# Attention scores accumulated by differences of key tiles, banks released one by one, an exponential placed behind the last Gelu

## The chip, the cores and the metric

The kernel runs on one core of a Trainium2 chip. The metric is the device time of one execution in microseconds, from launch to end; the profile's span is the time from the first to the last instruction and is a little shorter. The core has a matrix engine (TensorE, PE in the rows; PEld are its weight loads), a vector engine (VectorE, DVE), an activation engine (ScalarE, ACT), GpSimd (POOL) and SyncE (SP), which here issues all transfers. The engines run their own instruction lists and wait for each other through semaphores.

## What is computed

Two transformer layers on x of shape 4 x 1024 x 256, all in float32. The first layer is the one that most of the change touches:

```
x = x + attention_0(layernorm(x))     # 8 heads of 64, keys and values from a latent of 64
x = x + ffn_0(layernorm(x))           # silu gate, two hidden layers of 1024 with exact gelu
x = x + attention_1(layernorm(x))     # 16 heads of 16, rotary positions
x = x + ffn_1(layernorm(x))           # silu gate, 768 hidden
# attention_0:
scores = einsum('bqhd,bkhd->bhqk', q, k) * 64 ** -0.5
attn = softmax(scores, axis=-1)
out = einsum('bhqk,bkhd->bqhd', attn, v)
```

## The kernel before

There are two blocks of code. `attention_a` is the first attention, from 0 to about 787 us. `ffn_attention_ffn` holds the rest: it runs the first feed-forward layer block by block, the second attention, and the last feed-forward layer. The change touches `attention_a` in most places and the second block in one.

`attention_a` absorbs the key projection into the query, so all heads use the same latent of 64 numbers per token as keys. `Kh` and `Kl` hold it as a rounded high part and the rest (type fp32r, one pass on TensorE), for 1024 tokens of one of the 4 batches, in two copies, one for partitions 0 to 63 and one for 64 to 127, so that two heads run side by side. The same holds for the queries `Qh`, `Ql`.

The work is cut into units `u` (32 of them: 4 batches, 4 pairs of heads, 2 halves of 512 queries), each of 8 key tiles `t` of 128 keys, done in 4 pairs `j` (`t` = 2j and 2j+1). For each key tile:

- `scores(n)` (L969) makes keys x queries for both heads in the two banks of `psS[n % 2]`: four terms of two matmuls each, `Kh Qh`, `Kh Ql`, `Kl Qh`, and `spread` times `M`. The last subtracts the row's maximum: `M` has it in one row per head. Tile `t` uses the same two banks as tile `t-2`.
- `exponent(n)` on ScalarE (L589) makes `P` out of the banks; `weigh(n)` multiplies it with the values, in plain fp32; VectorE (`add`, L742, L746) and GpSimd (L885, L888, L892) add up `P` for the softmax's denominator.
- Six pairs ahead, `maxima(n)` (L945) makes queries x keys with the high parts alone in two banks of `psX`, and VectorE's `reduce(n)` (L709) takes the maximum over keys: with one instruction over two neighbouring banks (L720), or with two where the two banks are the last and the first (L722, L723).

`psX` has three banks that go round as a ring: `x_order` (L327) lists every user in the order of TensorE. A maximum takes two places (`double`), the others one: queries (in j=0), sums (end of j=1), rows and the output projection (j=2), and some more. A user waits until the one that had its bank before has released it. A double key had one release, when both heads had been reduced. The first 12 maxima partly use `psS`, which is still empty (`early_banks`).

In a pair TensorE's order is: a maximum, two key tiles of scores, the second maximum, the pending output projection (12 matmuls of 256 columns), the query (6 matmuls), latents and values of the next batch, `max_rows`, layer norm turns, then `weigh` for the two tiles of the pair before, and the sums. VectorE's order is: the first maximum, the additions of the pair before (L742 in j=3, L746 in j=0), one step on a weight tile (in turn, over four pairs: load, rounding on ScalarE, L771 which subtracts the rounded part, L774 which reduces it; from unit 22 on five steps with a cast L768), the second maximum, then what is left. The weight tile steps run on VectorE in j=1 and j=2 in the four-step form.

The denominator goes round through memory: sums on TensorE, a copy, a DMA, a reciprocal on VectorE in j=2, two DMAs, then GpSimd's `scale_out` (L876) on the output of that unit. The `wt` tiles in `shared` are weight buffers of the next block, filled by three loads at the end of SyncE's list in `attention_a` (L537).

In the second block ScalarE's list has, step by step `H`, the exponentials of the second attention (L1704), `leave(key)` for the feed-forward results (Silu at L1761, Gelu at L1765 and L1766, a scaled copy at L1770) and other copies. Where a function needs another table than the loaded one, an ACT_TABLE_LOAD stands in front of it.

## Time and profile before

| | us |
|---|---|
| median of the timed runs (three) | 2405.14 |
| lowest, highest | 2404.36, 2409.79 |
| the profiled execution | 2402.36 |
| its span | 2400.6 |
| TensorE busy | 2331.3 (97%) |
| VectorE busy | 1504.9 (63%) |
| ScalarE busy | 1342.5 (56%) |
| GpSimd busy | 1046.5 (44%) |

The shares are means over stages of different kinds; what a change in one stage is worth is read from that stage. The table of stretches gives for chosen stretches how long each engine was busy, with the number of instructions, then TensorE's granted clock as a part of full speed. The grouped instructions show, after the engine, operation, output and inputs, the count, the busy time, the mean of one in ns, and the idle time before them with the one that ended it. In a timeline a row begins with its start and its length; an idle time before it and its releaser stand in brackets. A row of matmuls marked x2 or x8 is several in one. TensorE's matmuls are pipelined and their ends are modelled, so the distance between starts tells what one costs, not its length.

### The profile page before, as it was taken

The page shows a single profiled execution, that of the slowest core. Times are in us where ns is not written, and L with a number is a line of the kernel's source. Part 1 is how long each engine was busy: PE and PEld are TensorE (multiplying, and loading weights), DVE is VectorE, ACT ScalarE, POOL GpSimd, SP SyncE. Part 2 cuts the span into 40 slices and gives each one's busy share as a digit, 9 for nine tenths or more (in the row PEclk, how much of TensorE's full clock was granted, in tenths as well). Part 3 has the DMA queues.
Part 4 walks back from the last instruction along what each step waited for, and adds up shares of the span by engine and source line. Part 5 has one row for each costly group of instructions (what it writes and reads, how often), then busy time and mean ns, then how long its engine had stood idle before and what let it go on. Part 6 is the DMA issues. An engine that isn't in the chain of part 4 may idle for free.

```text
span 2400.6 us, 39029 instructions
## 1 busy us (share of the span) xinstructions
PE 2331.3 (97%) x15265; PEld 1449.8 (60%) x15265; DVE 1504.9 (63%) x1938; ACT 1342.5 (56%) x1783; POOL 1046.5 (44%) x674
## 2 busy tenths in 40 slices
PE   6989999999999999999999999999999999999999
PEld 4545555555555788888888887444444444444588
DVE  6877777787784224322222223779989989989364
ACT  3555555554444444444444443478778778777743
POOL 1656776766677346556556556130000000000354
PEclk8999999999999999999999999999999999999999
DMA  2111321221212455565565556433333323322232
GB/s 61 63 69 54 98 79 56 98 65 61 73 44 69 149 167 181 176 196 184 172 197 185 173 188 201 128 90 80 88 79 72 86 77 75 90 79 55 61 121 80
DMA packets 156836, 259.04 MB, mean 108 GB/s; under 512 B 37004, under 2 KB 97292, under 8 KB 156300
## 3 DMA queue, kind: packets, MB, share of 16 engines
q1 hardware_dynamic: 156652, 256.53, 35.7%
q8 instruction: 123, 2.02, 0.3%
q14 instruction: 61, 0.50, 0.1%
HBM read 206.52 MB, written 60.68 MB: 111 GB/s over the span
## 4 chain that ended last, share of the span: by engine, by line
PE 62%; ACT 2%; DVE 1%; DMA 1%; issue 1%; SPq 1%; POOL 0%; POOLq 0%
PE m_R L129 46%; PE m_O L129 11%; PE m_X L129 4%; ACT m_P L1704 1%; DMA m_K<-bounce_k 1%; PE m_X L226 1%; ACT m_OS L1711 1%; DVE m_mraw L1853 0%; SPq L1562 0%; PE m_X L2067 0%; DVE m_ln_x L205 0%; PE m_R L226 0%; DMA inverses<-m_rinv 0%; DVE m_ln_stat L183 0%; SPq L1589 0%
## 5 line engine op out<-in xcount | busy, mean ns | idle before, releaser
L1853 DVE TENSOR_REDUCE m_mraw<-m_R 128x2 f32<-128x1024 f32 x512 | 622.6, 1221 | 71.1 <-PE m_R L129 57.6
L1704 ACT ACTIVATE m_P<-m_R 128x1024 f32<-128x1024 f32 x512 | 523.5, 1025 | 149.6 <-PE m_R L129 149.2
L589 ACT ACTIVATE a_P<-a_S 128x1024 f32<-128x1024 f32 x256 | 248.7, 1023 | 214.5 <-PE a_S L129 213.6
L129 PE MATMUL m_O<-m_P,m_V 128*17 128x256 f32 x4096 | 330.1, 394 | 4.5 <-ACT m_P L1704 2.6
L888 POOL TENSOR_TENSOR a_accp<-a_accp,a_P 128x1024 f32<-128x1024 f32 x96 | 251.9, 2624 | 15.3 <-ACT a_P L589 6.1
L1958 POOL TENSOR_TENSOR m_act0l<-m_xf,m_act0h 128x512 fp32r<-128x512 f32 x128 | 164.8, 1290 | 210.6 <-ACT m_xf L1766 111.2
L129 PE MATMUL a_O<-a_P,a_V 128*64 128x512 f32 x1024 | 247.7, 605 | 4.4 <-ACT a_ON L597 4.4
L129 PE MATMUL m_R<-m_act0h,wt 128*128 128x512 f32 x640 | 251.5, 393 | 0.0
L129 PE MATMUL m_R<-m_act0l,wt 128*128 128x512 f32 x640 | 250.4, 391 | 0.0
L720 DVE TENSOR_REDUCE a_mraw<-a_X 128x2 f32<-128x1024 f32 x164 | 199.7, 1218 | 79.6 <-PE a_X L129 79.5
L129 PE MATMUL m_R<-m_Q,m_K 64*128 64x512 f32 x800 | 200.6, 498 | 2.3 <-DVE m_mraw L1853 2.0
L129 PE MATMUL m_R<-m_act1l,wt 128*128 128x512 f32 x512 | 202.1, 395 | 0.0
L129 PE MATMUL m_R<-m_act1h,wt 128*128 128x512 f32 x512 | 200.8, 392 | 0.0
L129 PE MATMUL m_R<-m_K,m_Q 48*128 48x512 f32 x800 | 181.7, 450 | 4.8 <-ACT m_P L1704 3.7
L1982 POOL TENSOR_TENSOR m_ON<-m_ON,m_yt 128x512 f32<-128x512 f32 x16 | 20.5, 1283 | 377.0 <-DMA m_yt<-inverses 377.0
L129 PE MATMUL m_R<-next_hi,wt 128*128 128x512 f32 x424 | 168.9, 398 | 2.8 <-PEq L40 2.8
L129 PEld LDWEIGHTS m_O<-m_P,m_V 128*17 128x17 f32 x4096 | 85.3, 121 | 139.6 <-issue 130.0
L129 PE MATMUL m_R<-next_lo,wt 128*128 128x512 f32 x424 | 168.4, 397 | 0.0
L129 PEld LDWEIGHTS m_R<-m_Q,m_K 64*128 64x128 f32 x800 | 74.6, 183 | 151.2 <-issue 127.6
L129 PEld LDWEIGHTS m_R<-m_act0h,wt 128*128 128x128 f32 x640 | 120.2, 188 | 26.8 <-POOL m_act0l L1958 2.1
L129 PEld LDWEIGHTS m_R<-m_act0l,wt 128*128 128x128 f32 x640 | 120.3, 188 | 24.4 <-issue 0.5
L129 PE MATMUL a_X<-a_Kh,a_Qh 64*128 64x512 f32 x496 | 113.7, 450 | 19.2 <-DVE a_mraw L720 11.9
(251 smaller groups left out, 4235.0 us busy)
## 6 DMA issues: line engine op xcount, KB each, us to landing
wt<-wcopy SPq DMA_DIRECT2D x176, 512.0 KB, 3.4
m_K<-bounce_k SPq DMA_DIRECT2D x96, 128.0 KB, 5.4
m_ln_x<-x SPq DMA_DIRECT2D x23, 512.0 KB, 4.0
a_tile<-in_L_ffn_tiles SPq DMA_DIRECT2D x22, 512.0 KB, 4.5
wcopy<-in_L_ffn_tiles SPq DMA_DIRECT2D x22, 512.0 KB, 5.2
x<-xres SPq DMA_DIRECT2D x78, 128.0 KB, 3.2
m_Q<-bounce_q SPq DMA_DIRECT2D x150, 64.0 KB, 2.2
xres<-x SPq DMA_DIRECT2D x64, 128.0 KB, 2.6
```

The source lines that it names most:

```text
L129: return pe.eng.matmul(out, lhsT, rhs, start=start, stop=stop, skip_group_check=True)
L226: ins = pe.eng.transpose(bank[:, 128 * k:128 * k + 128], self.x[:, 4 * half + k, 128 * f:128 * f + 128], ident)
L589: act.eng.activation(P[n % NP][:, :, :], psS[n % 2][:, :, :], ACT.Exp, scale=SCALE).then_inc(s_exp)
L720: dve.eng.tensor_reduce(mraw[u % 2][:, t, :], psX[:, first:first + 2, :], AX.X, ALU.max).then_inc(X.free(key))
L888: pool.eng.tensor_tensor(accp[:, :, :], accp[:, :, :], P[n % NP][:, :, :], ALU.add).then_inc(s_addp)
L1704: act.eng.activation(P[h % 4][:, :, :], pair(key)[:, :, :], ACT.Exp, scale=SCALE).then_inc(R.free(key))
L1711: act.eng.activation(OS[:, :], psO[:, :], ACT.Copy).then_inc(s_os)
L1853: dve.eng.tensor_reduce(mraw[u % 2][:, at, :], pair(key)[:, :, :], AX.X, ALU.max).then_inc(R.free(key))
L1958: pool.eng.tensor_tensor(act_buf[dst][1][:, m, :], xf[fs(key) % 2][:, :], f32(act_buf[dst][0][:, m, :]), ALU.subtract).then_inc(s_lo)
L1982: pool.eng.tensor_tensor(ON[:, f, cols], ON[:, f, cols], yt[half][:, :], ALU.mult).then_inc(s_norm[half])
```

## The change

Three things. First, the scores of tiles t >= 2 are no longer made anew. `differ(b, half)` on TensorE makes K_t - K_{t-2} for tiles 2 to 7 of a batch, with the identity and its negative as weights: `half` 1 is 256 columns (tiles 6, 7), `half` 0 is 512 (tiles 2 to 5). ScalarE rounds it into `Dh`, which lies in the `wt` buffers, and VectorE writes the rest over `Kl`. `scores` then adds three terms to what stands in the banks since tile t-2, without the flag that starts a sum and without the `spread` term. For a later batch the two halves are made in j=3 of units 6 and 7 of the batch before; for the first, ahead of the loop. The loads into `wt` wait for the last scores that use the buffer. Second, a maximum has one ring key for each head, and VectorE reduces and releases each bank by itself. Third, a 4-column Exp is issued behind the last Gelu of the first feed-forward layer.

```diff
+    def differ_at(u, j):
+        b = u // UB + 1
+        return (b, {(6, 3): 1, (7, 3): 0}[u % UB, j]) if b < B and (u % UB, j) in ((6, 3), (7, 3)) else None
...
-            out += [("max", n), ("max", n + 1)] if n < STEPS else []
+            out += [("max", n + i, h) for i in range(2) for h in range(NH)] if n < STEPS else []
...
-        X = Ring(p, "x", 3, x_order(), double=("max",))
+        X = Ring(p, "x", 3, x_order())
...
+        Dh = [shared.wt[i][:, 0:T - 256] for i in (0, 1, 0, 2)]
...
+        def differ_cols(half):
+            return slice(768, T) if half else slice(256, 768)
+
+        def differ_back(half):
+            return slice(512, 768) if half else slice(0, 512)
...
             for i in range(3):
                 sp.wait_ge(s_copy, 16 * LOWS0)
+                sp.wait_ge(s_scores, (3 * UB * NT, 2 * UB * NT, STEPS)[i])
                 sp.eng.dma_start(f32(shared.wt[i][:, :]), wcopy[i]).then_inc(s_wt, 16)
...
+            def differ_high(b, half):
+                key, cols = ("differ", b, half), differ_back(half)
+                act.wait_ge(*X.filled(key))
+                if b >= 2:
+                    act.wait_ge(s_scores, NT * UB * (b - 1))
+                act.eng.activation(Dh[b][:, cols], differ_bank(key), ACT.Copy).then_inc(s_differ)
...
+            act.eng.activation(minus[:, :], ident[:, :], ACT.Copy, scale=-1.0).then_inc(s_identr)
...
+            def differ_low(b, half):
+                key, cols = ("differ", b, half), differ_cols(half)
+                dve.wait_ge(s_differ, 2 * b + 2 - half)
+                dve.eng.tensor_tensor(Kl[b % 2][:, cols], differ_bank(key), f32(Dh[b][:, differ_back(half)]), ALU.subtract).then_inc(X.free(key))
...
-                    dve.wait_ge(*X.filled(key))
-                    first = X.slot(key)
-                    if first < 2:
-                        dve.eng.tensor_reduce(mraw[u % 2][:, t, :], psX[:, first:first + 2, :], AX.X, ALU.max).then_inc(X.free(key))
-                    else:
-                        dve.eng.tensor_reduce(mraw[u % 2][:, t, 0:1], max_bank(n, 0), AX.X, ALU.max)
-                        dve.eng.tensor_reduce(mraw[u % 2][:, t, 1:2], max_bank(n, 1), AX.X, ALU.max).then_inc(X.free(key))
+                    for h in range(NH):
+                        key = ("max", n, h)
+                        dve.wait_ge(*X.filled(key))
+                        dve.eng.tensor_reduce(mraw[u % 2][:, t, h:h + 1], bank(key), AX.X, ALU.max).then_inc(X.free(key))
...
+            def differ(b, half):
+                key, here, back = ("differ", b, half), differ_cols(half), differ_back(half)
+                pe.wait_free(X, key)
+                pe.wait_ge(s_identr, 2)
+                for i in range(2):
+                    pe.wait_ge(*X.emptied(("latent", b, i)))
+                terms = [(identr[:, :], k[b % 2][:, here]) for k in (Kh, Kl)] + [(minus[:, :], k[b % 2][:, back]) for k in (Kh, Kl)]
+                products(pe, differ_bank(key), terms).then_inc(X.full(key))
...
                 if early_banks(n) is None:
-                    pe.wait_free(X, key)
+                    for h in range(NH):
+                        pe.wait_free(X, ("max", n, h))
...
-                terms = ((Kh[b % 2], cols, Qh[u % 3]), (Kh[b % 2], cols, Ql[u % 3]), (Kl[b % 2], cols, Qh[u % 3]), (spread, slice(0, 128), M[u % 3]))
+                if t < 2:
+                    terms = ((Kh[b % 2], cols, Qh[u % 3]), (Kh[b % 2], cols, Ql[u % 3]), (Kl[b % 2], cols, Qh[u % 3]), (spread, slice(0, 128), M[u % 3]))
+                else:
+                    for half in range(2):
+                        pe.wait_ge(*X.emptied(("differ", b, half)))
+                    since = slice(128 * t - 256, 128 * t - 128)
+                    terms = ((Dh[b], since, Qh[u % 3]), (Dh[b], since, Ql[u % 3]), (Kl[b % 2], cols, Qh[u % 3]))
                 for i, (w, c, x) in enumerate(terms):
                     for h in range(NH):
                         rows = slice(64 * h, 64 * h + 64)
-                        ins = mm(pe, psS[n % 2][:, h, :], w[rows, c], x[rows, :], i == 0, i == 3)
+                        ins = mm(pe, psS[n % 2][:, h, :], w[rows, c], x[rows, :], t < 2 and i == 0, i == len(terms) - 1)
...
+                    if key == ("hidden", NB - 1, 1, MT - 1):
+                        act.wait_ge(norm.s_half, 1)
+                        act.eng.activation(ready[:, :], norm.minus_half[:, :], ACT.Exp)
```

## Rows read from the trace of the kernel before

**Rows 1.** Table of stretches: length, then busy us of each engine, clock, DMA
```profile
200.00:560.00 360.00, 354.25 (x2286) 201.35 (x2282) 274.36 (x346) 191.67 (x252) 258.95 (x114) 1.00 0.24 77
560.00:700.00 140.00, 131.82 (x855) 73.91 (x857) 109.85 (x124) 66.27 (x85) 95.48 (x43) 1.00 0.21 65
```

**Rows 2.** Grouped instructions by shape, 25 to 755 us
```profile
L720 DVE TENSOR_REDUCE a_mraw<-a_X 128x2 f32<-128x1024 f32 x164 | 199.7, 1218 | 79.6 <-PE a_X L129 79.5
...
L129 PE MATMUL a_S<-a_M,a_spread 64*128 64x512 f32 x500 | 99.7, 391 | 0.0
...
L771 DVE TENSOR_TENSOR a_tile<-a_tile,a_tile_hi 128x1024 f32<-128x1024 f32 x22 | 38.8, 1762 | 4.8 <-ACT a_tile_hi L643 4.8
```

**Rows 3.** Timeline of TensorE over one unit: j=2, then j=3, 0, 1
```profile
300.96 0.50 PE L129 MATMUL a_X<-a_Kh,a_Qh 64*128 64x512 f32 x2
...
301.99 0.39 PE L129 MATMUL a_S<-a_M,a_spread 64*128 64x512 f32 x2
302.22 0.39 PE L129 MATMUL a_S<-a_Qh,a_Kh 64*128 64x512 f32 x2
...
303.68 0.28 PE L129 MATMUL a_X<-a_wo,a_osp1l 128*128 128x256 f32 x1
303.80 0.40 PE L129 MATMUL a_X<-a_wo,a_osp1h 128*128 128x256 f32 x2
...
307.19 0.50 PE L129 MATMUL a_X<-a_Kh,a_Qh 64*128 64x512 f32 x2
...
311.56 0.51 PE L129 MATMUL a_X<-a_Kh,a_Qh 64*128 64x512 f32 x2
...
314.66 0.63 PE L129 MATMUL a_X<-a_ln_hi,a_wq 128*128 128x512 f32 x2
...
317.55 0.50 PE L129 MATMUL a_X<-a_Kh,a_Qh 64*128 64x512 f32 x2
...
322.49 0.50 PE L129 MATMUL a_X<-a_Kh,a_Qh 64*128 64x512 f32 x2
```

**Rows 4.** Timeline of VectorE: one early place, then pair j=1 of that unit
```profile
89.33 3.04 DVE L771 TENSOR_TENSOR a_tile<-a_tile,a_tile_hi 128x1024 f32<-128x1024 f32 x1
...
318.09 1.23 DVE L720 TENSOR_REDUCE a_mraw<-a_X 128x2 f32<-128x1024 f32 x1 [0.98 <-PE a_X L129]
319.23 1.25 DVE L771 TENSOR_TENSOR a_tile<-a_tile,a_tile_hi 128x1024 f32<-128x1024 f32 x1
320.40 0.68 DVE L722 TENSOR_REDUCE a_mraw<-a_X 128x1 f32<-128x512 f32 x1
321.00 0.67 DVE L723 TENSOR_REDUCE a_mraw<-a_X 128x1 f32<-128x512 f32 x1
```

**Rows 5.** Waits of TensorE, 40 to 757 us: total, times, longest
```profile
PE a_X L129 <- DVE a_mraw L720: 12.3, 16, 1.8
```

**Rows 6.** Timelines ahead of the loop: VectorE, then TensorE
```profile
35.48 1.23 DVE L715 TENSOR_REDUCE a_mraw<-a_S 128x2 f32<-128x1024 f32 x1 [1.10 <-PE a_S L129]
...
40.20 0.80 PE L129 MATMUL a_X<-a_Kh,a_Qh 64*128 64x512 f32 x2 [2.64 <-DVE a_mraw L715]
```

**Rows 7.** Timelines: GpSimd's last addition of a unit, TensorE's sums of it
```profile
317.00 2.39 POOL L892 TENSOR_TENSOR a_accd<-a_accd,a_accp 128x1024 f32<-128x1024 f32 x1
...
321.93 0.64 PE L129 MATMUL a_X<-a_accd,a_ones 128*32 128x256 f32 x8
```

**Rows 8.** Timeline of TensorE: the closing sums of the first attention
```profile
772.67 1.08 PE L129 MATMUL a_X<-a_accd,a_ones 128*64 128x512 f32 x4 [0.70 <-issue]
```

**Rows 9.** Start of the second attention's exponentials: ScalarE, TensorE, the stretch
```profile
1528.93 1.28 ACT L1704 ACT_TABLE_LOAD   x1
1530.23 2.88 ACT L1704 ACTIVATE m_P<-m_R 128x1024 f32<-128x1024 f32 x3
...
1531.30 0.50 PE L129 MATMUL m_R<-m_K,m_Q 48*128 48x512 f32 x2 [1.75 <-ACT m_P L1704]
...
1530.00:1535.00 5.00, 3.51 (x20) 1.44 (x20) 2.90 (x4) 3.09 (x4) 0.00 (x0) 0.76 0.53 209
```

More of the change, by code:

```diff
@@ L331, in x_order @@
         for n in range(2 * AHEAD):
-            out += [("max", n)] if early_banks(n) is None else []
-            out += [("rows", 0)] if n == NT - 1 else []
+            out += [("max", n, h) for h in range(NH)] if early_banks(n) is None else []
+            out += [("differ", 0, 1), ("differ", 0, 0), ("rows", 0)] if n == NT - 1 else []
         pending = None
@@ L419, in bank, with differ_bank @@
             return psX[:, X.slot(key), :]
+        def differ_cols(half):
+            return slice(768, T) if half else slice(256, 768)
+        def differ_back(half):
+            return slice(512, 768) if half else slice(0, 512)
+        def differ_bank(key):
+            return bank(key)[:, 0:256] if key[2] else bank(key)
         def max_bank(n, h):
@@ L423, in max_bank @@
                 return psS[early_banks(n)][:, h, :]
-            return psX[:, (X.slot(("max", n)) + h) % 3, :]
+            return bank(("max", n, h))
         def p_freed_by_adds(n):
@@ L643, in tile_high @@
                 act.eng.activation(tile_hi[:, :], tile[:, :], ACT.Copy).then_inc(s_tile_hi)
+            for half in (1, 0):
+                differ_high(0, half)
             keep_rows(0)
@@ L817, in vector @@
                 reduce(n)
+                if n == NT - 1:
+                    for half in (1, 0):
+                        differ_low(0, half)
             pending = None
@@ L960, in maxima @@
                     ins = mm(pe, max_bank(n, h), Qh[u % 3][rows, 128 * q:128 * q + 128], kt[rows, 512 * kh:512 * kh + 512])
-                ins.then_inc(X.full(key) if early_banks(n) is None else s_early)
+                    if early_banks(n) is None:
+                        ins.then_inc(X.full(("max", n, h)))
+                if early_banks(n) is not None:
+                    ins.then_inc(s_early)
             def max_rows(u):
@@ L1048, in tensor @@
                 if n == NT - 1:
+                    for half in (1, 0):
+                        differ(0, half)
                     max_rows(0)
```

17 lines of the change are left out of this document (14 added, 3 removed).

## Prediction

> **What bounds the kernel now.** I read first the table of stretches. In the steady part of the first attention TensorE is busy 354.25 of 360 us at the full clock (1.00, the 2.4 GHz level), VectorE 274.36 (76%), ScalarE 53%, GpSimd 72%. In the stretch where weight tiles are cast (560 to 700 us) TensorE has fallen to 131.82 of 140 and VectorE is at 78% [rows 1]. So TensorE bounds this stage, with VectorE close behind. Next the grouped instructions: the term `spread`/`M` is 500 recorded matmuls, two per key tile (32 units of 8 tiles make 512) [rows 2]. Then the timeline. Two matmuls of the two heads run side by side: such a couple starts 0.23 us after the one before (301.99 to 302.22). From it come the lengths of the four pairs of a unit, by the first maximum of each: j=2 6.23 us (300.96 to 307.19), j=3 4.37, j=0 5.99, j=1 4.94, together 21.53 [rows 3]. Last, who waits for whom: between 40 and 757 us TensorE waited 12.3 us in 16 places for a whole maximum (L720) [rows 5]; these are the places where VectorE already rules.
>
> **The change part by part.**
>
> **Scores by differences.** From t=2 on a key tile adds (K_t - K_{t-2})Q to the bank that still holds the scores of t-2, whose subtracted maximum stays in it. Three couples are left of four. 6 of 8 tiles of 32 units are 192 tiles: 192 x 0.23 = **44.2 us** less TensorE work. Pairs j=1, 2, 3 lose 0.46 each, j=0 (t=0, 1) none. That this comes off the span holds only while TensorE is what ends last.
>
> **Making the differences.** Per batch `differ` adds four matmuls of 512 columns and four of 256, all with 128 rows. Two of the 512-column kind in a row take 0.63 us at 314.66, where one alone is 0.39 [rows 2, 3]: 0.23 to 0.24 for each more, as a couple. Two of 256 columns follow each other in 0.12 (303.68 to 303.80) [rows 3]. So 4 x 0.23 + 4 x 0.12 = 1.4 us, in three batches inside the loop 4.2 us. Ahead of it the engine changes from 64 to 128 rows, some 0.1, which the matmuls behind it paid before. ScalarE (two copies) is 53% busy and hides its part. VectorE gets two subtractions per batch, some 0.35 and 0.6 us, in j=3, where only the add L742 stands beside the maxima; the following maximum needs them at about 4.8 us of a pair that the same `differ` has lengthened, so nothing.
>
> **Before the loop** `differ(0)` falls between maximum 7 and `max_rows(0)`. VectorE is the bound there: TensorE waits 2.64 us for it at 40.20. But VectorE idles 1.10 us before 35.48 [rows 6]; the two subtractions (0.95) fit into most of that. Bounds -0.5 (a busier TensorE could leave the 1.2 GHz level earlier) to +1.5; I take +0.3.
>
> **Releasing banks singly.** 164 maxima that were one L720 of 1218 ns become two reductions [rows 2]; the other 84 after the early ones were already split. In the chain one L720 takes 1.14 (318.09 to 319.23) and a half 0.60 (320.40 to 321.00) [rows 4]: 0.06 more each, 10 us of VectorE. In return a bank is free 0.6 us earlier. That helps the second maximum of a pair, and the first of the next one only where no other user took a bank between them (j=3 to j=0). After j=0 the query, after j=1 the sums take the third bank, and both halves must be done. Of the 12.3 us [rows 5] I credit 1 us; bounds 0 and 5.
>
> **What becomes late next.** For VectorE in pair j=1: the first reduction starts 0.54 after the pair (318.09 against 317.55), 1.20 for it, then `tile - tile_hi` (L771), then 1.20. With 1.17 us for L771 as at 319.23 that ends at 4.11, and the pair now has 4.94 - 0.46 = 4.48: in time. But L771 averages 1762 ns [rows 2], with 3.04 us at 89.33 [rows 4]: at 1.76 the end is at 4.70, 0.22 late, where before it had 0.24 spare. In j=3, with the add L742 at the 1.17 of an undisturbed operation of this shape and only the first half awaited: 0.54 + 1.20 + 1.17 + 0.60 = 3.51 against 3.91, in time. In j=2 there is more than 1 us of room, and j=0 is as before. About 24 units at 0.2 are 5 us; where the cast makes a five-step cycle (six units, TensorE waiting already) I add 2 us. Together 7 (bounds 0 and 15).
>
> What the trace shows of L771: 1.25 us at one place and 3.04 at another for the same shape [rows 4]. The Trainium skill's page "SBUF — State Buffer", in its section on who interferes with whom, says that a VectorE instruction with two SBUF inputs and a GpSimd instruction that reads SBUF exclude each other. By that rule, the trace agrees: L771, L742 and L746 are of that kind, and a reduction from PSUM is not. It does not say how often they will meet after the change.
>
> **GpSimd's loop.** `rinv` lands, GpSimd scales and adds, its last add L892 starts at 317.00 and ends at 319.39, and TensorE's sums want it at 321.93: 2.5 us spare [rows 7]. The landing follows a reciprocal whose place on VectorE is in j=2. Of the 1.38 us that a unit loses, about 1.4 can come off this spare; 1.1 stay. No cost.
>
> **SyncE.** The loads of `wt` now wait for the last scores; they stand behind the last inverse anyway. The residual loads queued behind them wait with them, for nothing new. In the last unit the closing sums wait 0.70 us at 772.67 for GpSimd's last add [rows 8], whose start hangs on the inverse of the unit before; so the saving of the last pair (0.46) is lost.
>
> **The exponential behind the last Gelu.** The table load at 1528.93 takes 1.28 us with the second attention's first exponential ready behind it (1530.23), and TensorE waits 1.75 us until 1531.30 for that; the granted clock falls to a mean of 0.76 in those 5 us, so part of them ran at 1.2 GHz [rows 9]. Moved to an idle ScalarE, 1.28 is won, up to 1.75, plus up to 0.9 if the clock stays up. I take 1.7.
>
> The page "ScalarE: Activation LUTs" of the Trainium skill, section "What ACT_TABLE_LOAD costs", puts a switch at about 2.66 us, a drain of 1.38 included. Here the load begins as the copy before it ends and 1.3 us later the exponential runs [rows 9], so the drain is not seen; by the page the total would be 1 us lower still.
>
> **The sum.** -44.2 + 0.5 + 4.2 + 0.3 - 1 + 7 - 1.7 = **-34.9 us**. The profiled execution took 2402.4 us (span 2400.6 and 1.8 around it), which makes 2367.5; it was 2.8 us faster than the median of the timed runs, 2405.1, so against that I forecast **2370 us**.
>
> **The rivals.**
> 1. *TensorE stays the bound and the single banks clear the waits* (15%). The 7 us don't come and 5 of the old waits go: -44.2 + 0.5 + 4.2 - 5 - 1.7 = -46, 2359 us. For it: 24% idle time on VectorE in the steady part, waits of TensorE there of only a few us in all. Against: the pairs are uneven, and VectorE's work per pair is too.
> 2. *VectorE takes over in j=1 and j=3* (15%). Its work per unit, 21.53 x 0.76 = 16.4 us, becomes 17.0 of 20.15, 84%, and everything that makes one pair late is handed to the next. Then two of three savings are lost: 29.5 back, -44.2 + 29.5 + 0.5 + 4.2 + 0.3 - 1.7 = -11.4, 2394 us. Halfway to it is 2382.
> 3. *Slower: VectorE and GpSimd collide in every unit* (4%). The place is L771 in j=1, the price its 3.04 us (2.97 in the chain) in place of 1.17, and the halves not overlapping (0.68 in place of 0.60) because each now has a wait of its own: 0.54 + 1.36 + 2.97 + 1.36 = 6.23 against 4.48, 1.75 us in each of 29 units, +51. With -41 from the rest that is +10: 2415 us. It decides from an L771 of about 2.8 us on in every unit. Against: the mean over all of them is 1.76 us [rows 2].
> 4. *The change doesn't do all it says*: a copy behind the moved exponential brings the old table back, so the load returns at its old place. Copies run between exponentials in the first attention without a load, so I give it 3%: 2372 us, inside the forecast.
>
> **How the numbers follow.** Forecast 63%, rivals 15, 15, 4 and 3%. The range takes in rival 1 and the way to rival 2, with the bound of the late pairs (15): 2358 to 2388. What a measurement of this kernel can tell from no change is about 0.2%, 5 us. Faster by more than that 0.94 (all but rival 3 and the worst end of rival 2), within it 0.03, slower 0.03.
>
> **What would show each step.** The group of `spread` falls from 500 to about 128 matmuls and the couple spacing stays 0.23. j=3 of the unit near 300 us lasts 3.9, j=0 still 6.0. TensorE's waits for the two reduction lines in the first attention lie between 15 and 30 us; above 40 is rival 2. L892 still ends before the sums want it. The second attention's first exponential starts within 0.2 us of the scores before it, with no load between. Wrong would be: a spacing of a couple above 0.25, a unit longer than 20.8 in the steady part, or VectorE without idle time in j=1.

## The result and the profile after

| | us | against before |
|---|---|---|
| before, median of eight timed runs | 2404.75 (2401.76 to 2409.79) | |
| changed kernel, median of eight | 2386.43 (2378.05 to 2393.43) | ratio 0.9918, 95% interval 0.9907 to 0.9929 |
| changed kernel, profiled execution | 2388.71, span 2386.9 | |

By the ratio the change saves 19.7 us (17.1 to 22.4). The forecast was 35 us, 2370; the time lies inside its range of 2358 to 2388, 1.6 us from the upper end, and past the halfway point to rival 2 (2382). So the direction was right and nearly half of the gain did not come. The profiles are one execution each: by them the change is worth 13.7 us, since the profiled execution before was 2.4 us faster than its median and the one after 2.3 us slower, so a difference of a few us between two profiles can be noise. One of the five timed runs of e7 below took 3511 us at a granted clock of 0.56; it is left out of the ratio (without it the median is 2377.9).

To see where the gain is missing, I cut every profiled execution at three events that both kernels have: the last output copy of the first attention's 32 units, the start of the next block (its first table load), and the first exponential of the second attention.

| part of the profiled execution, us | before | after | difference | forecast |
|---|---|---|---|---|
| units of the first attention | 770.4 | 753.4 | -17.0 | -33.7 |
| its closing sums and output | 18.6 | 21.2 | +2.6 | +0.5 |
| first feed-forward layer | 741.3 | 738.8 | -2.5 | -1.7 |
| second attention to the end | 870.4 | 873.6 | +3.2 | 0 |

Nearly all that is missing is missing in the units. The table of stretches shows both sides of it (length, then busy us with the count for TensorE, its weight loads, VectorE, ScalarE, GpSimd; then the granted clock). The changed kernel, an early stretch and the two of [rows 1]:

```profile
60.00:155.00 95.00, 87.12 (x520) 45.31 (x516) 84.45 (x122) 48.05 (x62) 59.33 (x27) 1.00 0.20 67
...
200.00:560.00 360.00, 347.21 (x2164) 193.33 (x2162) 292.18 (x441) 195.67 (x260) 261.93 (x116) 1.00 0.25 80
560.00:700.00 140.00, 128.34 (x785) 70.46 (x786) 115.97 (x163) 67.30 (x87) 97.70 (x45) 0.98 0.20 62
```

The kernel before in the same early stretch, of which the forecast had quoted one row (89.33 in [rows 4]) and no busy time:

```profile
60.00:155.00 95.00, 90.86 (x560) 47.99 (x558) 78.19 (x98) 46.67 (x59) 57.68 (x26) 1.00 0.20 68
```

In the steady part VectorE rose from 274 to 292 busy us of 360 (81%), and TensorE fell from 354 to 347: some of its work went, and part of the room stayed empty. In the early stretch VectorE was at 82% already and went to 89%; TensorE stands idle for 8 us of 95. The last stretch has a granted clock of 0.98 where it was 1.00 before; what stands behind that is shown with e7. Next, who waits for whom (total us, times, longest), TensorE between 40 and 757 us, changed kernel; it answers to [rows 5]:

```profile
PE a_X L129 <- DVE a_mraw L755: 26.3, 38, 2.2
PE a_O L129 <- ACT a_ON L622: 7.3, 4, 2.3
PE a_X L226 <- DVE a_mraw L755: 4.9, 6, 1.4
```

The same view of the kernel before has, beside the 12.3 us of [rows 5]:

```profile
PE a_O L129 <- ACT a_ON L597: 4.4, 4, 1.6
PE a_X L129 <- DVE a_mraw L723: 4.0, 8, 0.8
...
PE a_X L226 <- DVE a_mraw L723: 2.5, 2, 1.5
PE a_X L226 <- DVE a_mraw L720: 1.9, 2, 1.0
```

So the waits for maxima went from 20.7 (12.3 + 4.0 + 2.5 + 1.9) to 31.2 (26.3 + 4.9), just above the 15 to 30 that the forecast named, and those for ScalarE's copy of a finished output from 4.4 to 7.3. The groups that answer to [rows 2], 25 to 755 us of the changed kernel (count, busy us, mean ns, idle before):

```profile
L755 DVE TENSOR_REDUCE a_mraw<-a_X 128x1 f32<-128x512 f32 x496 | 317.9, 682 | 93.3 <-PE a_X L129 92.5
...
L804 DVE TENSOR_TENSOR a_tile<-a_tile,a_tile_hi 128x1024 f32<-128x1024 f32 x22 | 43.2, 1965 | 5.4 <-ACT a_tile_hi L669 5.4
L129 PE MATMUL a_S<-a_M,a_spread 64*128 64x512 f32 x128 | 25.7, 393 | 0.0
```

`spread` fell from 500 to 128 as forecast. L804 is L771 of before: its mean rose from 1762 to 1965 ns.

### The profile page after: what moved, and what is told of

Read it like the earlier page. It is cut to its first block, busy times and chain, and to the rows that moved or that the text cites. A ratio compares the mean times of both kernels' runs of the same rounds, so it can differ in the third digit from the quotient of the medians.

```text
span 2386.9 us, 38698 instructions
## 1 busy us (share of the span) xinstructions
PE 2302.6 (96%) x14913; PEld 1425.2 (60%) x14913; DVE 1532.2 (64%) x2110; ACT 1346.0 (56%) x1793; POOL 1045.0 (44%) x674
## 4 chain that ended last, share of the span: by engine, by line
PE 61%; ACT 2%; DMA 2%; DVE 1%; issue 1%; SPq 1%; POOL 0%; POOLq 0%; ACTq 0%
PE m_R L129 45%; PE m_O L129 10%; PE m_X L129 4%; DMA m_K<-bounce_k 1%; ACT m_P L1766 1%; PE m_X L226 1%; SPq L1624 1%; DVE m_mraw L1918 1%; ACT m_OS L1773 0%; DVE m_ln_x L205 0%; PE m_X L2132 0%; PE m_R L226 0%; DMA bounce_k<-m_comp 0%; DMA inverses<-m_rinv 0%; ACT m_comp L1786 0%
## 5 line engine op out<-in xcount | busy, mean ns | idle before, releaser
L755 DVE TENSOR_REDUCE a_mraw<-a_X 128x1 f32<-128x512 f32 x496 | 317.9, 682 | 93.3 <-PE a_X L129 92.5
L926 POOL TENSOR_TENSOR a_accp<-a_accp,a_P 128x1024 f32<-128x1024 f32 x96 | 249.5, 2599 | 13.7 <-ACT a_P L614 4.5
```

The lines of the kernel that those rows point to most:

```text
L755: dve.eng.tensor_reduce(mraw[u % 2][:, t, h:h + 1], bank(key), AX.X, ALU.max).then_inc(X.free(key))
L926: pool.eng.tensor_tensor(accp[:, :, :], accp[:, :, :], P[n % NP][:, :, :], ALU.add).then_inc(s_addp)
```

## The unit near 300 us, beside the forecast

Timeline of TensorE in the changed kernel (start, length), one couple of each pair's first and second maximum and a few between:

```profile
294.60 0.50 PE L129 MATMUL a_X<-a_Kh,a_Qh 64*128 64x512 f32 x2 [0.21 <-DVE a_mraw L755]
294.91 0.43 PE L129 MATMUL a_S<-a_Qh,wt 64*128 64x512 f32 x2
295.14 0.42 PE L129 MATMUL a_S<-a_Ql,wt 64*128 64x512 f32 x2
295.37 0.42 PE L129 MATMUL a_S<-a_Qh,a_Kl 64*128 64x512 f32 x2
...
296.45 0.49 PE L129 MATMUL a_X<-a_Kh,a_Qh 64*128 64x512 f32 x2
296.96 0.39 PE L129 MATMUL a_X<-a_wo,a_osp1h 128*128 128x256 f32 x1
...
300.70 0.50 PE L129 MATMUL a_X<-a_Kh,a_Qh 64*128 64x512 f32 x2
...
302.42 0.39 PE L129 MATMUL a_X<-a_Kh,a_Qh 64*128 64x512 f32 x2
...
304.61 0.51 PE L129 MATMUL a_X<-a_Kh,a_Qh 64*128 64x512 f32 x2
...
310.60 0.50 PE L129 MATMUL a_X<-a_Kh,a_Qh 64*128 64x512 f32 x2
...
315.40 0.50 PE L129 MATMUL a_X<-a_Kh,a_Qh 64*128 64x512 f32 x2 [0.25 <-DVE a_mraw L755]
```

The three terms of a tile (294.91, 295.14, 295.37) stand 0.23 apart: a couple that adds to a bank with old contents costs what another does. The four pairs last 6.10 (300.70 - 294.60), 3.91, 5.99 and 4.80. The forecast for TensorE alone was 5.77, 3.91, 5.99 and 4.48. j=3 and j=0 are exact. j=1 is 0.32 late, of which 0.25 is listed as a wait for VectorE. Timeline of VectorE in that pair:

```profile
311.13 1.29 DVE L755 TENSOR_REDUCE a_mraw<-a_X 128x1 f32<-128x512 f32 x2 [0.97 <-PE a_X L129]
312.34 1.72 DVE L804 TENSOR_TENSOR a_tile<-a_tile,a_tile_hi 128x1024 f32<-128x1024 f32 x1
313.98 1.27 DVE L755 TENSOR_REDUCE a_mraw<-a_X 128x1 f32<-128x512 f32 x2
```

It is the chain of the forecast: 0.53 after the pair starts, then 1.21, then 1.64 for L804, then the second maximum. j=2 is 0.33 late, where the forecast saw over 1 us of room; no wait is listed inside it. The gaps tell: 0.51 from the second maximum (296.45) to the output projection (296.96), where before it is 0.33 (303.13 to 303.46). VectorE was late there:

```profile
294.69 0.75 DVE L183 BATCH_NORM_STATS2 a_ln_stat<-a_ln_x 128x6 f32<-128x256 f32 x2
295.48 0.25 DVE L186 BATCH_NORM_AGGREGATE a_ln_mv<-a_ln_stat 128x2 f32<-128x6 f32 x2
295.64 1.26 DVE L755 TENSOR_REDUCE a_mraw<-a_X 128x1 f32<-128x512 f32 x2
296.82 1.21 DVE L807 TENSOR_REDUCE a_lows<-a_tile 128x1 f32<-128x1024 f32 x1
```

Layer norm statistics of the pair before are still running when j=2 starts, so the first reduction begins 1.04 us behind the start of the pair instead of 0.54. The statistics alone don't do it: in e4 below, where the subtraction in j=1 is short, the same statistics end at 284.56, the first reduction (284.79) waits for TensorE, and the pair takes 5.59. In five of 22 units between 230 and 706 us j=2 is that long (6.08 to 6.10); in the others of the plain kind it is 5.59 to 5.67, under the forecast's 5.77. The forecast took the 6.23 of before as TensorE's own time, but some 0.18 of it was a wait that no list shows: without VectorE's load (e5) the same pair lasts 6.05. A plain unit of the second and third batch thus takes 20.3 to 20.9 us, where before it is 21.5 and TensorE alone would need 20.0 (shown below). That is 0.9 saved of 1.4 on average, and the longest (20.91 and 20.92) meet one of the forecast's signs of being wrong, a unit over 20.8. The four units around a change of batch save less: of 22.77, 27.74, 23.39 and 21.54 us (from 322 us on, before) 0.29, 0.28, 0.72 and 0.34 are gone. From batch to batch the end of the last unit moves by 3.8, 4.5, 4.5 and 4.2 us, where the forecast has 8.4 each on average, and 9.9 without its losses.

## The experiments

Medians in us; the ratio is to the kernel before on the same chip, with its 95% interval. Line numbers are those of the changed kernel. An edit is shown cut where dots stand.

| | edit | us | ratio |
|---|---|---|---|
| e1 | before + exponential | 2402.26 | 0.9979 (0.9966 to 0.9991) |
| e2 | before + single banks | 2399.36 | 0.9974 (0.9962 to 0.9985) |
| e3 | changed, double banks | 2403.57 | 0.9984 (0.9974 to 0.9994) |
| e4 | changed, light weight tiles | 2361.59 | 0.9811 (0.9798 to 0.9825) |
| e5 | before, light weight tiles | 2391.22 | 0.9931 (0.9916 to 0.9945) |
| e6 | changed, tile step last | 2381.42 | 0.9892 (0.9876 to 0.9907) |
| e7 | changed, output copy first | 2378.40 | 0.9876 (0.9860 to 0.9893) |
| e8 | e6 and e7 | 2378.52 | 0.9870 (0.9851 to 0.9889) |
| e9 | changed, light reduction only | 2377.99 | 0.9879 (0.9863 to 0.9895) |
| e10 | changed, one-input operations | 2389.84 | 0.9935 (0.9922 to 0.9948) |
| e11 | e7, tile steps a pair earlier | 2389.79 | 0.9939 (0.9920 to 0.9958) |
| e12 | before, output copy first | 2405.43 | 1.0001 (0.9992 to 1.0010) |

**The parts singly.** e1 is the kernel before with the 4-column Exp alone:

```diff
+                    if key == ("hidden", NB - 1, 1, MT - 1):
+                        act.wait_ge(norm.s_half, 1)
+                        act.eng.activation(ready[:, :], norm.minus_half[:, :], ACT.Exp)
```

> The kernel before with only the exponential behind the last Gelu. My sum says 1.3 to 2.6 us less (1.7 taken). In its profile the second attention's first exponential starts with no table load before it, and the clock of the five microseconds behind it stays at 1.00 instead of 0.76. If the changed kernel's missing gain lies here (a later wait takes it back), the time is that of the kernel before within 0.5 us.

e2 is the kernel before with one ring key for each head and two reductions, so the second part of the diff alone:

```diff
...
-        X = Ring(p, "x", 3, x_order(), double=("max",))
+        X = Ring(p, "x", 3, x_order())
...
```

> The kernel before with only the maximum's two banks released singly. Theory V (what the changed kernel lost, VectorE's path between two maxima takes): the kernel before has 16 us of waits of TensorE for a maximum, most with another user of the bank between them, so -3 to +1 us. Theory R (the split itself is the harm, 10 us more of VectorE and a second wait in each maximum): +5 to +15 us, and most of the 20 us that are missing from the forecast's 39 are explained.

e3 is the reverse: the changed kernel with a maximum as one double key again (that line and the reductions turned back), so the differences and the exponential alone.

> The changed kernel with the maxima as before: one key over two banks, one reduction and one release where the banks are neighbours. Differences and exponential stay. Theory V: without the 0.6 us earlier release the waits at j=3 to j=0 and inside the pairs come on top, 3 to 10 us slower than the changed kernel, so 10 to 17 us faster than before. Theory R: faster than the changed kernel by 5 to 15 us, 25 to 35 us faster than before.

Measured: e1 saves 5.0 us (2.2 to 8.2), e2 6.3, e3 3.8; all together save 19.7. e2 gave more than expected and e3 less than either theory; e1's interval reaches its 1.3 to 2.6. The exponential alone is worth no less than e3, so **the differences without single banks are worth nothing measurable** (-1 us, give or take 4), and 10 us of the result belong to no part alone (19.7 - 3.8 - 6.3). The release, which the forecast credited with 1 us, is worth 6 by itself and 16 on top of the differences. Of the 6, e2's profile shows the place: j=2 of a plain unit lasts 6.04 instead of 6.24 us, the wait named above, and the units end 4.7 us earlier (765.7 instead of 770.4). What the release removes behind the differences stands in TensorE's timeline of e3, pairs j=1 and j=2 of the unit near 300:

```profile
295.56 0.50 PE L129 MATMUL a_X<-a_Kh,a_Qh 64*128 64x512 f32 x2
...
297.53 0.50 PE L129 MATMUL a_X<-a_Kh,a_Qh 64*128 64x512 f32 x2
...
300.40 0.50 PE L129 MATMUL a_X<-a_Kh,a_Qh 64*128 64x512 f32 x2
...
302.39 0.50 PE L129 MATMUL a_X<-a_Kh,a_Qh 64*128 64x512 f32 x2
```

From first to second maximum it is 1.97 and 1.99 us; with single banks 1.72 (300.70 to 302.42 above). Between them stand two tiles of scores, and these are what the change shortens: 2.17 us before (300.96 to 303.13), 1.71 after. The second maximum needs a bank of the first. With a double key that is free only at 0.54 + 1.2, plus the way to TensorE, about 1.97: with four couples per tile it was in time by 0.2, with three it is late by 0.26. Over half of the 0.46 that such a pair saves goes there, and 0.11 more behind it: the step from the second maximum to the next matmul is 0.43 (302.39 to 302.82) where a maximum in time has 0.32. A unit of the second batch in e3 takes 21.1 to 21.3 us, 0.3 less than before, and making the differences takes back a part of that; its units end 3.4 us earlier (767.0).

**VectorE's work.** In e4 and e5 the two steps that VectorE does on each of 27 weight tiles work on 8 of 1024 columns. That is work left out; the rest stands.

```diff
-                    dve.eng.tensor_tensor(low[:, :], tile[:, :], f32(tile_hi[:, :]), ALU.subtract).then_inc(s_tile_lo)
+                    dve.eng.tensor_tensor(low[:, 0:8], tile[:, 0:8], f32(tile_hi[:, 0:8]), ALU.subtract).then_inc(s_tile_lo)
...
-                    dve.eng.tensor_reduce(lows[:, n:n + 1], low[:, :], AX.X, ALU.max, apply_absolute_value=True).then_inc(s_low)
+                    dve.eng.tensor_reduce(lows[:, n:n + 1], low[:, 0:8], AX.X, ALU.max, apply_absolute_value=True).then_inc(s_low)
```

> The changed kernel, in which VectorE's two steps on a weight tile (subtract the rounded part, reduce) work on 8 of the 1024 columns: the test for inexact weights then sees only those columns. 54 long operations of VectorE go, some 80 us of its busy time, and with them what meets GpSimd in j=1. Theory V: units of the second batch fall from 20.9 us on average to 20.15, those of the first batch from 22.5 to near 20.5, and the kernel is 12 to 20 us faster than the changed one, at about 2368. A rival (TensorE's couples became dearer, or GpSimd's loop is the bound): not more than 3 us faster than the changed kernel.

> Control for the lightened run: the kernel before with the same two VectorE steps on 8 of 1024 columns (the test for inexact weights sees only those). Theory V: TensorE has 16 us of waits for maxima to lose here, so -8 to -18 us against before, and the differences together with the single banks are then worth the difference to the lightened changed kernel (-44 us), 27 to 36 us, close to the 38 that the couples and the differences come to. The rival (the lightening itself is worth the same 25 us in both kernels): 25 us less here, so that the change is worth no more than 19 us also without the load.

Measured: the lightening is worth 26 us in the changed kernel and 17 in the one before (by ratios: 0.9918 - 0.9811, and 1 - 0.9931). Against each other (0.9931 - 0.9811) the change is worth 29 us without that load, 19.7 with it, so by the timed runs the load takes 9 us of it, give or take 6. e5 came as expected, e4 gave more than the 12 to 20. In the profiles the units end 32.6 us earlier in e4 (727.3) than in e5 (759.9). A plain unit lasts 19.96 in e4 (5.59, 3.90, 5.99, 4.48) and 21.34 in e5 (6.05, 4.36, 5.99, 4.94): **exactly 0.46 less in each of the three pairs**. The term of 0.23 a tile is right wherever VectorE is in time. TensorE's waits of e4:

```profile
PE a_X L129 <- DVE a_mraw L755: 9.5, 15, 1.7
PE a_O L129 <- ACT a_ON L622: 7.3, 4, 2.3
```

By batch, the end of the last unit moves by these steps: 9.3, 6.9, 7.2 and 9.2 us from e5 to e4, against 3.8, 4.5, 4.5 and 4.2 from before to after. By these four profiles the load takes 15.6 us of the change's worth: 5.5 in the first batch, 5.0 in the last, and 2.4 and 2.7 in the two steady ones that the forecast reasoned from. That is more than the 9 of the timed runs, as the profiled pair before and after lies close together by chance (13.7 against 19.7 us), and 3.2 us of the last batch are two falls of the clock, shown with e7. The lightened kernels don't lose the waits for GpSimd either: the group of the subtraction in e4:

```profile
L804 DVE TENSOR_TENSOR a_tile<-a_tile,a_tile_hi 128x8 f32<-128x8 f32 x22 | 20.1, 914 | 5.4 <-ACT a_tile_hi L669 5.4
```

e9 leaves only the reduction of those steps on 8 columns (work left out), 27 operations of 1.2 us:

```diff
-                    dve.eng.tensor_reduce(lows[:, n:n + 1], low[:, :], AX.X, ALU.max, apply_absolute_value=True).then_inc(s_low)
+                    dve.eng.tensor_reduce(lows[:, n:n + 1], low[:, 0:8], AX.X, ALU.max, apply_absolute_value=True).then_inc(s_low)
```

> The changed kernel in which only the second of the two weight tile steps on VectorE, the reduction in j=2, works on 8 of 1024 columns (the test for inexact weights sees only those). The subtraction in j=1, the one that GpSimd's reads can hold up, stays whole. 27 operations of 1.21 us go. If the harm is VectorE's amount of work, half of the 25 us that both steps gave comes, 10 to 15. If the harm is the subtraction in j=1 and its collisions, as my forecast had it, 2 to 8 us.

e10 keeps both steps' length but not their two inputs: two reductions of 1016 columns into a spare column, and subtraction and reduction on 8 columns (their result on the others is left out):

```diff
-                    dve.eng.tensor_tensor(low[:, :], tile[:, :], f32(tile_hi[:, :]), ALU.subtract).then_inc(s_tile_lo)
+                    dve.eng.tensor_tensor(low[:, 0:8], tile[:, 0:8], f32(tile_hi[:, 0:8]), ALU.subtract)
+                    dve.eng.tensor_reduce(spare[:, 2 * n:2 * n + 1], tile[:, 8:1024], AX.X, ALU.max).then_inc(s_tile_lo)
...
-                    dve.eng.tensor_reduce(lows[:, n:n + 1], low[:, :], AX.X, ALU.max, apply_absolute_value=True).then_inc(s_low)
+                    dve.eng.tensor_reduce(spare[:, 2 * n + 1:2 * n + 2], tile[:, 8:1024], AX.X, ALU.max)
+                    dve.eng.tensor_reduce(lows[:, n:n + 1], low[:, 0:8], AX.X, ALU.max, apply_absolute_value=True).then_inc(s_low)
```

> The changed kernel with both weight tile steps at full length but without an operation that reads two SBUF tensors: the subtraction and the last reduction work on 8 columns, and a reduction of the tile itself over the other 1016 columns, 1.2 us whose result nobody uses, stands beside each (the test for inexact weights sees only 8 columns). VectorE's count of long steps stays, the collisions of the subtraction with GpSimd go. If collisions are the harm, 10 to 20 us less than the changed kernel. If the amount of VectorE's work is, within 5 us of it.

Measured: e9 is 8 to 9 us faster than the changed kernel (by medians, by ratios, give or take 5) for 32 us of VectorE's work, e10 3 to 4 slower (give or take 4). e9 falls between the two ranges that were expected of it. So the reductions alone, at one input and 1.2 us each, cost about a quarter of their length: amount matters. e10 was to show what meetings with GpSimd cost, and it is not clean. Its groups (count, busy us, mean ns):

```profile
L805 DVE TENSOR_TENSOR a_tile<-a_tile,a_tile_hi 128x8 f32<-128x8 f32 x22 | 18.8, 856 | 5.4 <-ACT a_tile_hi L670 5.4
...
L810 DVE TENSOR_REDUCE a_lows<-a_tile 128x1 f32<-128x8 f32 x22 | 3.4, 153 | 0.0
```

A subtraction of 8 columns still averages 856 ns where a reduction of 8 takes 153. The 0.7 between them does not come from its size, so e10 kept that wait. How much of the late pairs is amount and how much is meeting stays open.

**Order on VectorE and ScalarE.** e6 moves the tile step behind the second maximum of its pair:

```diff
-                if tile_at(u, j):
-                    tile_low(*tile_at(u, j))
                 if ahead < STEPS:
                     reduce(ahead + 1)
...
+                if tile_at(u, j):
+                    tile_low(*tile_at(u, j))
                 if judge_at(u, j) is not None:
```

> The changed kernel with the weight tile's step as the last thing VectorE does in a pair, behind the second maximum, query, residual and the rest, in place of between the two maxima. All work stays. Theory V with the place as the cause (a long step between the maxima delays the second, on which the next pair's first hangs): j=1 falls from 4.8 us to 4.5, the collisions cost less, and the kernel gets 6 to 15 us faster than the changed one. If VectorE's amount of work per unit is the bound, the order gives nothing: within 3 us of the changed kernel.

e7 moves ScalarE's copy of a finished output, in j=0, ahead of a layer norm scaling and a tile's rounding. e12 is the same edit on the kernel before.

```diff
+                if j == 0 and u:
+                    keep_out(u - 1)
                 if norm_at(u, j) and norm_at(u, j)[1] >= 5:
...
                     tile_high(tile_at(u, j)[0])
-                if j == 0 and u:
-                    keep_out(u - 1)
```

> The changed kernel with ScalarE's copy of the finished output (keep_out) ahead of the layer norm's scaling and the weight tile's rounding in j=0. In the changed kernel TensorE waited 2.35, 2.00 and 1.95 us for this copy once per batch, and behind the first and the last of these its eight matmuls took 3.5 and 3.6 us in place of 1.94. Expected: these waits fall below 0.5 us and the matmuls stay at 1.94, 6 to 9 us less. If the scaling only moves behind and makes the turns late instead: within 3 us.

> The changed kernel with both moves, the weight tile's step last on VectorE and the output's copy first on ScalarE. If their causes are apart the gains add: 10 to 22 us less than the changed kernel, 2364 to 2376 us. If they share the wait (the copy is late only because VectorE is), no more than the larger of the two.

> Control for the run with the output's copy first on ScalarE: the same move in the kernel before. TensorE waited there 4.4 us for the copy in four places, with no fall of the clock behind them (1.94 us for the eight matmuls). If the 9 us in the changed kernel came from longer waits and the clock behind them, here it is 1 to 5 us; if the move is good for 9 in any case, 7 or more.

e11 is e7 with the weight tiles' steps one pair earlier, so that the subtraction falls in j=0:

```diff
-    LOWS0, LOWS, LOW_FIRST = 22, 27, 3
+    LOWS0, LOWS, LOW_FIRST = 22, 27, 2
```

> The changed kernel with the output's copy first on ScalarE (as in the run of that alone, 9 us better than the changed kernel) and the weight tile's four steps one pair earlier: subtraction in j=0, reduction in j=1, load in j=2. Pair j=1 then has 0.54 + 1.20 + 1.13 + 1.20 = 4.07 us of VectorE up to the end of its second maximum against 4.48 of TensorE, in time; j=0 has the add and the subtraction together, 0.54 + 1.20 + 1.4 + 1.2 + 1.2 = 5.5 against 5.99 without a collision, 7 or more with two. If collisions are rare, 2365 to 2372 us, the best version that keeps all of the work. If GpSimd's last additions, which run in j=0, meet both, slower than the run with the copy alone, 2380 or more.

Measured: e6 is 5 to 6 us faster than the changed kernel (by medians, by ratios; TensorE waits 16.9 instead of 26.3 for the maxima), at or under the least that was expected of it; e7 is 8 to 10 faster, both together (e8) no more than e7, and e12 is no change. A reason why e6 brings little is in its pair lengths: j=1 is at 4.48, but the step now stands in front of the next pair's first maximum, and the median of j=2 is 6.02 us, in e8 6.41, where the changed kernel has 5.67. What e7 went after stands in TensorE's timeline of the changed kernel:

```profile
157.10 3.50 PE L129 MATMUL a_O<-a_P,a_V 128*64 128x512 f32 x8 [2.35 <-ACT a_ON L622]
...
335.44 1.94 PE L129 MATMUL a_O<-a_P,a_V 128*64 128x512 f32 x8 [2.00 <-ACT a_ON L622]
...
511.83 3.63 PE L129 MATMUL a_O<-a_P,a_V 128*64 128x512 f32 x8 [1.95 <-ACT a_ON L622]
```

and in its table of stretches around the last:

```profile
510.00:517.00 7.00, 5.17 (x26) 1.81 (x27) 3.03 (x5) 5.01 (x9) 5.15 (x4) 0.76 0.00 0
```

After waits of 2.35 and 1.95 us the next eight matmuls take 3.50 and 3.63 us; the same eight take 1.94 elsewhere. The granted clock of the stretch is a mean of 0.76, between the levels of 1.2 and 2.4 GHz. So these two waits cost 4.3 us and 3.2 more for the clock. It does not always fall: behind the 2.00 us at 335.44 the eight took 1.94, and in e10, with waits of 2.35, 1.95 and 1.95 us at the same three places, all three times. The first of them:

```profile
156.08 1.94 PE L129 MATMUL a_O<-a_P,a_V 128*64 128x512 f32 x8 [2.35 <-ACT a_ON L623]
```

The clock of the changed kernel fell in two more places of the units, behind waits for VectorE. The first:

```profile
630.35 0.50 PE L129 MATMUL a_X<-a_Kh,a_Qh 64*128 64x512 f32 x2 [2.16 <-DVE a_mraw L755]
...
633.26 2.66 PE L129 MATMUL a_O<-a_P,a_V 128*64 128x512 f32 x8
```

From 629 to 635 us the granted clock is a mean of 0.72, and so it is from 674 to 680, behind a wait of 2.03 at 674.86. The pairs j=1 that begin there last 6.06 us each; in e7, with waits of 2.12 and 1.75 before them and no fall, 4.47. That is 3.2 us again. The kernel before has no such fall between 50 and 770 us; its longest wait in the loop is 1.8.

In e7 the place of 511.83 reads:

```profile
510.29 1.94 PE L129 MATMUL a_O<-a_P,a_V 128*64 128x512 f32 x8
```

All four waits for the copy (7.3 us) are gone in e7, but not all of that is won: TensorE comes sooner to the next maximum and waits there, 1.68 us at 514.48, and in the first batch:

```profile
160.60 0.50 PE L129 MATMUL a_X<-a_Kh,a_Qh 64*128 64x512 f32 x2 [3.69 <-DVE a_mraw L755]
```

Its waits for maxima are 34.0 us instead of 31.2. By batch, the last unit's end moves by +0.9, -1.1, -2.3 and -5.6 us from the changed kernel to e7, and more than half of that last step is the two falls of the clock that e7's profile doesn't have. So the waits for the copy are gone (shown), but how much of the 8 us is theirs, and how much is a clock that fell less often, isn't separated. In e12 the four waits of before (4.4, longest 1.6) are gone too. A wait of 2.91 us for a maximum stands at 163.17 instead. e12's units end 2.8 us earlier in the profile (767.6), the second attention is 3.0 longer (873.4), and the timed runs show nothing where 1 to 5 us were expected. No clock fell behind the shorter waits of before. e11 is 11 to 15 us slower than e7, as expected for the case that GpSimd meets both operations. TensorE's waits for L755 are 41.6 + 3.4 us, up to 2.6 long. The group of the subtraction in e11:

```profile
L804 DVE TENSOR_TENSOR a_tile<-a_tile,a_tile_hi 128x1024 f32<-128x1024 f32 x22 | 51.8, 2355 | 0.0
```

In j=0 VectorE has an addition of its own (L779) and GpSimd scales and adds (from 305.88 in the unit above): 2355 ns instead of the 1902 of e7. The amount of work is the same; 0.45 us more in each of 22 are 10 us, near the 11 to 15 that were lost.

**The best version** that leaves nothing out is e7 or e8, which can't be told apart: 2378.4 and 2378.5 us, ratios 0.9876 and 0.9870, some 30 us under the kernel before and 8 to 12 under the changed one.

## Why the prediction was right or wrong

- **Bound.** TensorE as the bound, VectorE close behind: right for the steady part. It was read from 200 us on, and of batch 0 only one row of VectorE; there VectorE was at 82% already, and 89% after.
- **44.2 us from 192 tiles at 0.23.** Right as TensorE's work: 19.96 against 21.34 in e4 and e5, spacing 0.23, `spread` 128. j=3 at 3.91 and j=0 at 5.99 are as forecast in the changed kernel too.
- **Making the differences**, 1.4 a batch. The timeline gives from the second maximum to the values' matmuls 1.45 (395.40 to 396.85) and 0.98 (374.69 to 375.67), where without them 0.32 stands (302.42 to 302.74), so 1.79 a batch: three batches 5.4 instead of 4.2.
- **Releasing banks singly**, 1 us. This is the step that failed in its reasoning. It was priced on the waits that the kernel before shows [rows 5], which are few because the second maximum comes 2.17 us behind the first. The first part of the change moves that to 1.71, and then the whole reduction (about 1.97, e3) is late. It is worth 6 us on before and 16 behind the differences. The sum took the 44.2 as granted and the kernel had both parts, so this mistake cost the total nothing, and that was luck: the forecast had one part worth 40 and one worth 1, and in the runs the first is worth nothing measurable without the second.
- **Late pairs**, 7 us with bounds of 0 and 15. Too small, though by how much is uncertain. j=1 was late by 0.32 (0.22 forecast); j=2, given over 1 us of room, was late by 0.33 in five units, where L804 in j=1 had pushed the statistics in front of its first reduction. The weight tiles' steps cost the change 9 us by the timed runs (give or take 6) and 15.6 by the profiles (e4 and e5), two thirds of that in batch 0 and in the batch with casts. It isn't all that is missing: without that load the change gives 29 us, where the sum without the 7 has 42. Those 12 or 13 us lie outside this term, in the points on ScalarE, the clock, the last unit and the second attention. The mean of 1.76 for L771 hid that it is long where it hurts: in batch 0 it meets GpSimd, 3.04 at 89.33 [rows 4]. After the change the place is the same. VectorE, then GpSimd, then TensorE:

```profile
87.06 3.06 DVE L804 TENSOR_TENSOR a_tile<-a_tile,a_tile_hi 128x1024 f32<-128x1024 f32 x1
```

```profile
86.67 2.37 POOL L923 TENSOR_TENSOR a_accp<-a_P 128x1024 f32<-128x1024 f32 x1
```

```profile
91.46 0.50 PE L129 MATMUL a_X<-a_Kh,a_Qh 64*128 64x512 f32 x2 [1.56 <-DVE a_mraw L755]
```

  The subtraction ends 1.08 us after GpSimd's operation does (90.12 against 89.04), so nearly all of the 1.25 of an undisturbed one [rows 4] lies behind it. The rule of the Trainium skill's page "SBUF — State Buffer" (who interferes with whom) that these two exclude each other for a whole instruction agrees with that, and so does e4: there the subtraction of 8 columns at the same kind of place (106.92) takes 2.02 us, 1.04 less than the 3.06 of 1024 columns (109.59), so the wait stayed and only the work went.
- **ScalarE** was only considered for the new copies, and everything else on it was put at nothing. Its copy of the output, which the change doesn't touch, went from 4.4 to 7.3 us of waits, and behind two of them the clock fell: about 6 us by these rows (2.9 + 3.2); moving it brought 8 to 10 (e7). In e4 it is the largest part of what is still missing there: j=1 with the wait for this copy lasts 7.65 and 7.45 us, where e5 has 6.19 and 6.18.
- **The clock** in the units was not in the sum. It fell four times in the profile of the changed kernel and not once before: 6.4 us. With nearly the same three waits for the copy it fell behind none in e10 and behind all three in e9, so this share differs between profiles.
- **Before the loop** +0.3: TensorE's first maximum of the loop comes at 40.64 instead of 40.20, but in e1 and e12, which don't change this part, it comes at 40.7, so no cost can be told from noise.
- **GpSimd's loop**, 1.1 us to spare. Right: its last addition near 300 ends at 312.97 and the sums start at 314.51.
- **The last unit**, +0.5. The cause was seen, its size was not: 2.6 us in that part. The closing sums in TensorE's timeline of after answer to [rows 8]:

```profile
756.83 1.23 PE L129 MATMUL a_X<-a_accd,a_ones 128*64 128x512 f32 x4 [1.89 <-issue]
```

  The wait grew from 0.70 to 1.89. GpSimd's last addition starts at 754.39, behind the landing of the inverse, and lasts 2.34. Most of the other 1.4 is the clock (0.73 from 754 to 762 us): the eight matmuls of the sums take 2.9 us instead of 1.9; in e4, e6 and e7, where they run at the full clock, the part takes 19.8 to 19.9.
- **The exponential**, 1.7 us. The steps happened as forecast. ScalarE and then TensorE at the place that answers to [rows 9], with the stretch:

```profile
1503.50 1.28 ACT L1885 ACT_TABLE_LOAD   x1
...
1513.35 2.93 ACT L1766 ACTIVATE m_P<-m_R 128x1024 f32<-128x1024 f32 x3
...
1514.42 0.50 PE L129 MATMUL m_R<-m_K,m_Q 48*128 48x512 f32 x2 [0.33 <-ACT m_P L1766]
```

```profile
1513.00:1518.00 5.00, 4.35 (x36) 1.67 (x32) 4.27 (x5) 4.03 (x5) 0.00 (x0) 1.00 0.87 334
```

  The load lies in idle time, the wait is 0.33 instead of 1.75, and the clock stays at its full level where before it was a mean of 0.76. Over all profiles the feed-forward part averages 738.9 with it and 740.4 without: 1.5 us. The timed comparison e1 says 5.0 (2.2 to 8.2), and no row shows the rest. That stays open.
- **Second attention to the end**, forecast without change: +3.2 us in the profile. TensorE's wait for the keys' transfer there was 0.5 before and is 3.9 now, once 1.9 long; nothing in the change touches these transfers. The same part takes 871.7 to 877.8 in the variants that carry the whole change and 869.7 to 873.4 in the others. It eats the 3 us, and its cause is open.
- **The rivals.** The result lies two thirds of the way from the forecast to rival 2. The bound of rival 2, waits over 40 us, was not reached (31.2). Rival 1's mechanism exists, 10 us of interplay, but sits inside the 44.2. Rival 3's price (3.06 for the subtraction) was met in batch 0, and 3.39 at 625.62 in the last batch (before: 3.40 at 639.60), in front of the wait at 630.35; elsewhere it stayed under 2.8. Rival 4 is out: every part does what it says.

In the units the account is: forecast without losses -39.7, measured -17.0, so 22.7 lost. Listed are 10.5 more of waits for maxima, 2.9 for the copy, 6.4 for the clock (3.2 behind the copy, 3.2 behind two maxima) and 1.2 for the differences: 21.0. The other 1.7 are of the size of gaps like that of 0.51 at 296.45, which lists of waits leave out.

The forecast came out right by 1.6 us at the edge of its range. What held was the bound, the 44.2 and the direction; the upper end was set by the late pairs alone, and what filled it was also the copy on ScalarE, the clock and the second attention, for which the sum had no term. That the total stayed inside is in part luck.

## What to carry to other kernels

Where a change makes one engine's stretch shorter than another's whole instruction, price the release of the buffer between them for the new length and not by the waits seen before: a saving can be worth nothing until its partner is in. Read the busy shares of every stage of the loop, the first one too, since a mean over a steady part (76%) said nothing of the batch where VectorE was at 82%. And after TensorE gets shorter, look through the other engines' lists for a release that stands behind work with no hurry: moving ScalarE's copy brought 8 us here, and nothing in the kernel before. Compare timed runs before you trust a difference between two single profiles: here they gave 13.7 us where eight runs each gave 19.7.

## What was not expected of the hardware

- A wait of about 2 us on TensorE can cost more than itself, and doesn't always: behind 1.95 and 2.35 us the next eight matmuls took 3.63 and 3.50 us instead of 1.94 and the stretch's granted clock was 0.76, behind 2.00 in the same run and behind 2.35, 1.95 and 1.95 in e10 they took 1.94.
- A two-input VectorE operation on SBUF of 8 columns averages 856 ns beside a busy GpSimd (e10; 914 in e4), a one-input reduction of 8 columns 153. Making such an operation small does not take its wait away.
- Accumulating on a bank that ScalarE has read in between costs nothing extra: 0.23 us per couple, as with the first term of a new sum.
